# Router and shared-gate logits from two matmul passes, with high and low gate weights side by side in one stationary operand

## The reference, cut to what matters

```
x = x + 0.5 * ffn(layernorm(x))        # first feed-forward
x = x + attention(layernorm(x))        # 16 heads of 128, causal
x = x + 0.5 * ffn(layernorm(x))        # second feed-forward, same weights
```

```
gu = x @ shared_gate_up_w.T ; g, u = split(gu)
shared = sigmoid(x @ shared_gate_w.T) * (silu(g) * u @ shared_down_w.T)
logits = x @ gate_w.T                  # 8 columns; the 9th is x @ shared_gate_w.T
top_w, top_i = top_k(softmax(logits), 2) ; top_w /= sum(top_w)
out = sum over the 2 experts of top_w * expert(x) + shared
```

## Time and profile before

| what | value |
|---|---|
| runs | 551.32, 553.97, 550.83 us |
| profiled execution | 550.31 us in all, span of its instructions 548.4 us |
| TensorE (PE) busy | 518.0 us, 94% of the span, 3318 matmuls |
| weight loads (PEld) busy | 459.2 us, 84% |
| VectorE (DVE) busy | 329.4 us, 60% |
| ScalarE (ACT) busy | 273.7 us, 50% |
| GpSimd (POOL) busy | 274.4 us, 50% |
| mean granted TensorE clock | 0.993 |

### The profile page before, as it was taken

One profiled execution on the slowest core, in us unless ns is written; L12 is line 12 of the kernel. 1 busy time (PEld: TensorE's weight loads), 2 busy tenths in 40 slices (PEclk: granted clock), 3 DMA queues, 4 the chain that ended last, 5 costly groups with the idle time before them and its releaser, 6 DMA issues. The chain is left out here.

```text
span 548.4 us, 10499 instructions
## 1 busy us (share of the span) xinstructions
PE 518.0 (94%) x3318; PEld 459.2 (84%) x3319; DVE 329.4 (60%) x821; ACT 273.7 (50%) x731; POOL 274.4 (50%) x364
## 2 busy tenths in 40 slices
PE   7999699986999999999999999999999899899995
PEld 4787699975898889888988988889889688799985
DVE  6689655558763564655545636646556768755536
ACT  3973355531663553653545525636446465355540
POOL 1738777752656434552654455435532321667750
PEclk9999799999999999999999999999999999999999
DMA  8941233353101002002010020020000140223336
GB/s 284 343 133 30 67 98 106 100 174 76 36 0 59 20 2 77 0 0 76 0 56 21 0 76 0 0 76 0 0 1 0 31 151 2 68 87 104 97 109 210
DMA packets 19401, 37.99 MB, mean 69 GB/s; under 512 B 2864, under 2 KB 10416, under 8 KB 19376
## 3 DMA queue, kind: packets, MB, share of 16 engines
q1 hardware_dynamic: 14960, 25.61, 14.4%
q0 software_dynamic: 4416, 12.06, 6.9%
HBM read 28.49 MB, written 9.18 MB: 69 GB/s over the span
## 5 line engine op out<-in xcount | busy, mean ns | idle before, releaser
L1317 POOL TENSOR_TENSOR s_a<-s_a,rr_a 128x128 f32<-128x128 f32 x64 | 25.6, 401 | 128.3 <-DVE rr_a L1413 128.3
L1353 ACT ACTIVATE s_a<-s_a,mn_a 128x128 f32<-128x128 f32 (+1 forms) x128 | 57.1, 448 | 27.9 <-DVE mn_a L1407 27.0
L179 PE MATMUL bank<-xT_h,area_h 128*128 128x512 f32 x128 | 55.3, 432 | 4.3 <-PEq L1171 3.4
L1403 DVE SCALAR_TENSOR_TENSOR s_a<-bank,cst 128x384 f32<-128x384 f32 x64 | 35.3, 552 | 34.4 <-PE bank L1524 34.4
L1419 DVE SCALAR_TENSOR_TENSOR area_l<-bank,bias_a,area_h 128x256 fp32r<-128x256 f32 x64 | 30.9, 482 | 41.2 <-ACT area_h L1363 41.1
L521 POOL DMA_INDIRECT xn<-x_normed,tok_i_f x46 | 45.7, 994 | 17.2 <-issue 10.5
L1363 ACT ACTIVATE area_h<-bank,bias_a 128x256 fp32r<-128x256 f32 x64 | 30.3, 473 | 42.2 <-PE bank L1552 41.1
L180 PE MATMUL bank<-xT_l,area_h 128*128 128x512 f32 x128 | 50.2, 392 | 0.0
L181 PE MATMUL bank<-xT_h,area_l 128*128 128x512 f32 x128 | 50.2, 392 | 0.0
L1551 PE MATMUL bank<-pT_a,v_a 128*128 128x256 f32 x128 | 39.8, 392 | 4.6 <-ACT pT_a L1358 4.6
L1395 DVE TENSOR_SCALAR qk_a<-bank,bias_a 128x512 f32<-128x512 f32 x32 | 24.0, 751 | 30.5 <-PE bank L181 30.5
(11 more groups left out here) (176 smaller groups left out, 1652.4 us busy)
## 6 DMA issues: line engine op xcount, KB each, us to landing
area<-in_wqkv SPq DMA_DIRECT2D x8, 768.0 KB, 4.4
xn<-y_by_token SPq DMA_DIRECT2D x12, 256.0 KB, 3.7
w_r<-in_w SPq DMA_DIRECT2D x8, 352.0 KB
area_r<-in_w SPq DMA_DIRECT2D x16, 176.0 KB
x_normed<-xn SPq DMA_DIRECT2D x4, 512.0 KB, 5.6
area<-in_wo SPq DMA_DIRECT2D x8, 256.0 KB, 2.7
x_res<-in_x_in SPq DMA_DIRECT2D x4, 256.0 KB, 4.2
wgu_r<-in_wgu SPq DMA_DIRECT2D x4, 256.0 KB
```

The lines of the kernel that those rows point to most:

```text
L179: pe.matmul(psum, lhs[0], rhs[0], start=first, stop=False)
L1353: act.activation(s[b][:, cols], s[b][:, cols], ACT.Exp, bias=mn[:, b, t:t + 1], scale=-1.0, accum_out=rs[:, b, t:t + 1]).then_inc(s_e, 1)
L1403: dve.scalar_tensor_tensor(s[b][:, :], bank[3 + u % 2][:, 0:3 * P], -INV_SCALE, cst[:, C_MASK:C_MASK + 3 * P], ALU.mult, ALU.max).then_inc ...
```

## The change

The gate weights become one tile, `wg_hl`, with four groups of 32 columns for each chunk: high, low, high, zero. Per chunk one matmul takes columns 0 to 63 (high and low side by side) against the high part of x, and one takes columns 64 to 127 (high and zeros) against the low part. Both add into the same 64 partitions of bank 6, so that rows 0 to 8 hold high by high plus high by low, and rows 32 to 40 hold low by high. That makes 4 matmuls per call of `logits`, each with 64 columns in its stationary operand, in place of 6 with 128. ScalarE copies 64 rows in place of 9. `route_turn` is no longer 8 transposes: each is a plain FP32 matmul with the 64x128 block of logits as stationary operand and a 64x9 matrix of zeros and ones as moving operand (`C_SUM`, in the constants), which turns and adds the two row groups in one. The constants grow by 9 columns; VectorE makes low parts for 32 columns per chunk in place of 128.

```diff
+GL = 32
...
-C_N = C_MASK + 3 * P
+C_SUM = C_MASK + 3 * P
+C_N = C_SUM + NG
...
+    for g in range(NG):
+        c[[g, GL + g], C_SUM + g] = 1.0
...
-        wg_h = sbuf("wg_h", [P, KD, P], FP32R)
-        wg_l = sbuf("wg_l", [P, KD, P], FP32R)
+        wg_hl = sbuf("wg_hl", [P, KD, 4 * GL], FP32R)
...
-                        act.activation(flat(wg_h[:, :, :]), wg_raw, ACT.Copy).then_inc(s_gh, 1)
+                        act.activation(wg_hl[:, :, :], wg_raw, ACT.Copy).then_inc(s_gh, 1)
...
-                            act.activation(lgT[2 * half + a][0:NG, :], bank[6][0:NG, a * D:(a + 1) * D],
+                            act.activation(lgT[2 * half + a][0:2 * GL, :], bank[6][0:2 * GL, a * D:(a + 1) * D],
                                            ACT.Copy).then_inc(s_lgt_sb, 1)
...
-                        dve.tensor_tensor(flat(wg_l[:, :, :]), wg_raw, flat(wg_h[:, :, :]).bitcast(FP32),
-                                          ALU.subtract).then_inc(s_gl, 1)
+                        dve.tensor_tensor(wg_hl[:, :, GL:2 * GL], wg_raw[:, :, GL:2 * GL],
+                                          wg_hl[:, :, GL:2 * GL].bitcast(FP32), ALU.subtract).then_inc(s_gl, 1)
...
                         for k in range(KD):
-                            last = split_matmuls(pe, bank[6][:, :], (wg_h[:, k, :], wg_l[:, k, :]),
-                                                 (xT_h[:, k, toks], xT_l[:, k, toks]), k == 0, k == KD - 1)
+                            pe.matmul(bank[6][0:2 * GL, :], wg_hl[:, k, 0:2 * GL], xT_h[:, k, toks],
+                                      start=k == 0, stop=False)
+                        for k in range(KD):
+                            last = pe.matmul(bank[6][0:2 * GL, :], wg_hl[:, k, 2 * GL:4 * GL], xT_l[:, k, toks],
+                                             start=False, stop=k == KD - 1)
                         last.then_inc(s_lgt, 1)
...
                         for j in range(NT):
-                            last = pe.transpose(bank[4][:, j * NG:(j + 1) * NG],
-                                                lgT[j // 2][0:NG, (j % 2) * P:(j % 2 + 1) * P],
-                                                cst[0:NG, C_ID:C_ID + NG])
+                            last = pe.matmul(bank[4][:, j * NG:(j + 1) * NG],
+                                             lgT[j // 2][0:2 * GL, (j % 2) * P:(j % 2 + 1) * P],
+                                             cst[0:2 * GL, C_SUM:C_SUM + NG], start=True, stop=True)
                         last.then_inc(s_logits, 1)
...
-    gate = np.concatenate([a["ffn_gate_w"], a["ffn_shared_gate_w"], np.zeros((P - NG, D), np.float32)], 0)
+    gate = np.concatenate([a["ffn_gate_w"], a["ffn_shared_gate_w"], np.zeros((GL - NG, D), np.float32)], 0)
+    gate = np.concatenate([gate, gate, gate, np.zeros_like(gate)], 0)
```

More of the change, by code:

```diff
@@ L31 @@
 NG = NE + 1
+GL = 32
+assert NG <= GL
 NH, DH = 16, 128
@@ L263, in ffn @@
                 w2_r = area_r[0:IC, :].rearrange("p (e c d) -> p e c d", e=NE, c=2)
-                wg_tile = sb("wg_tile", [P, max(KD * P, TOP_K * NT * NM)])
-                wg_raw = wg_tile[:, 0:KD * P]
+                wg_tile = sb("wg_tile", [P, max(KD * 4 * GL, TOP_K * NT * NM)])
+                wg_raw = wg_tile[:, 0:KD * 4 * GL].rearrange("p (k g) -> p k g", k=KD)
                 tile_hot = wg_tile[:, 0:TOP_K * NT * NM].rearrange("p (a b) -> p a b", b=NM)
@@ L453, in _ @@
                         sp.dma_start(cst[:, 0:C_DESC], consts[:, 0:C_DESC]).then_inc(s_cst, 16)
-                        sp.dma_start(wg_raw, wgate).then_inc(s_gate_in, 16)
+                        sp.dma_start(wg_tile[:, 0:KD * 4 * GL], wgate).then_inc(s_gate_in, 16)
                     for q, (src, raw, _, _) in enumerate(jobs):
@@ L1636 @@
         "consts": constants(),
-        "wgate": chunks(gate.T, D, P).reshape(P, KD * P),
+        "wgate": chunks(gate.T, D, P).reshape(P, KD * 4 * GL),
         "wgu": gu,
```

## The result

The changed kernel takes 554.88 us (median of 17 runs, 553.70 to 558.15); the kernel before, beside it on the same chip, takes 551.80 us (17 runs, 549.27 to 555.17). The ratio is 1.0054 with a 95% interval of 1.0035 to 1.0074: slower by 3.0 us (1.9 to 4.1). The forecast was 552.9 us, 1.8 us slower, in a range of 550.6 to 555.4. The time lies in the range; the sign is right and the size is 1.2 us short. By ratio it sits right on the line of 0.5% between "no change" and "slower".

What follows compares the result with a forecast made beforehand. TensorE was taken to bound the kernel around the turn. Per feed-forward -0.27 (first logits) - 0.08 (second) + 1.26 (turn) = +0.91 us, twice +1.8; from 551.1 that gives 552.9 us, range 550.6 to 555.4.

Steps and rivals of the forecast that it cites:

- What bounds the kernel: TensorE is busy throughout around the route turn, so what it loses or gains there shows at the end.
- Route turn: Sixteen FP32 loads 0.11 us apart plus 0.09 us: 1.85 us for 0.59, so +1.26 us per feed-forward.
- pace of the transposes: Rival at the turn: loads 0.062 us apart, 1.08 us for the turn; +0.3 us in all, 551.4; chance 0.08.
- no load pulled ahead: Rival at the turn: 0.21 us per load, 3.36 us for the turn; +4.8 us in all, 555.9; chance 0.1.
- `logits(1)`: Second logits call: the turn waits for ScalarE's copies, so only 0.08 us is gained per feed-forward.
- `logits(0)`: First logits call: the way in is free, the way out costs 0.19 us; 0.27 us gained per feed-forward.
- shape change by columns: At the logits: each switch between 128 and 64 stationary columns empties the array and costs 0.19 us.
- 0.3 us or more: Sign of shape changes: first matmul of `logits(1)` starts at least this long after its predecessor.
- the first rival: No change of shape by columns at the logits: +1.4 us in all, 552.5 us; chance 0.2.
- a new fall elsewhere: Clock rival: the granted clock falls at another place, giving 556 us; chance 0.04.

Runs made afterwards that it cites:

- e4: Changed kernel with each of the turn's eight FP32 matmuls issued twice; 586.64 us, ratio 1.0165 to the kernel before.
- e8: Changed kernel with all 128 columns in the logits matmuls and all 128 rows in the turn; 586.34 us, ratio 1.0095 to the kernel before.
- e2: Changed kernel with narrow logits kept, but the turn by transposes and VectorE adding the halves; 576.71 us, ratio 0.9964 to the kernel before.
- e6: Changed kernel with the turn two matmuls later in `shared_up(3)`; 581.96 us, ratio 1.0031 to the kernel before.
- e5: Changed kernel unaltered, timed again on another chip; 584.28 us, ratio 1.0072 to the kernel before.
- e3: Changed kernel with 64 moving columns in place of 9 at the turn; 579.70 us, ratio 1.0029 to the kernel before.
- e12: Kernel before, unaltered, profiled again on another chip; 577.75 us in one execution.
- e7: Changed kernel with narrow logits, turn by transposes, VectorE adding the halves, turn two matmuls later; 577.73 us, ratio 0.9953 to the kernel before.
- e9: Changed kernel with 64 moving columns at the turn and each turn matmul issued twice; 586.97 us, ratio 1.0151 to the kernel before.

## Why the prediction was nearly right, and what was mis-sized

That the time lies in the range is luck in part. The upper bound of 555.4 us was built from dearer loads and dearer shape changes, which did not come. What did come, a fall of the clock behind the turn, was in no term of the sum, and as a rival it stood outside the range (556); with it behind both turns in every execution the sum would be 551.1 + 4.6 = 555.7 us, outside.

- **What bounds the kernel: right.** The turn and the work around it set the end. f0's delay came to the first expert product in full behind an unchanged wait of 4.14 us, as the steps of the earlier trace rows said. That part of it went again in this execution, between 61 and 120 us, is due to where the low clock lay.
- **Route turn: right.** 1.88 us for 1.85, 0.111 us a load for 0.11, and 0.09 us beyond the loads as predicted (e4); 0.07 of these go when the operand has all 128 rows (e8). The rivals "pace of the transposes" (1.08 us) and "no load pulled ahead" (3.36 us) fell. The Trainium skill, "Perfetto Trace Analysis", section Transposes, asks to do a logical transpose with the transpose operation and not with a standard matmul. The runs agree and give the price: 1.88 against 0.64 us for the same eight blocks (the changed kernel and e2).
- **`logits(1)`: right.** From the first matmul of `shared_up(2)`'s second group to the turn, 4.31 us became 4.22, so 0.09 us were gained (0.08 predicted), and TensorE now waits 0.30 and 0.26 us for ScalarE. e6 shows the lost 0.3 us by getting it back.
- **`logits(0)`: the shape change by columns, which I priced at 0.19 us, costs nothing.** From the first logits to the first matmul behind them it took 1.44 us and takes 0.93, 0.51 us less and not 0.27; and the first matmul of `logits(1)` starts 0.23 us behind its predecessor (23.29 to 23.52), where the prediction had named 0.3 us or more as its sign. I had carried the loss of the earlier trace rows, where rows change, over to columns. This was the first rival (chance 0.2), and it makes the work +0.7 us per feed-forward in place of 0.91: +1.4 in all. The rule of the Trainium skill that I weighed there ("TensorEngine Tiling (Array Packing)", section Key Properties: a change of the tiling mode drains the engine) is not borne out for 64 columns: the loads at 23.29 and 24.20 run ahead of their matmuls. No row says whether an operand of 64 columns puts the array in another mode at all. For 64 rows the rule agrees with the earlier trace rows. The prediction put the delay behind the turn down to the shape too; e8 and the attention's rows show that most of it stands there at full shape as well. It is there before and after the change, so the sum does not suffer.
- **The clock: the term that was missing, +1.6 us.** I had given "a new fall elsewhere" a chance of 0.04 as a mishap. It belongs to the change: 16 loads in a row, with nearly nothing behind each, are followed by a stretch at half clock in 6 of 12 cases, 1.6 us each. With a rate of a half that is 2 x 0.5 x 1.6 = +1.6 us, and 1.4 + 1.6 = 3.0 us is what was measured. How well the two agree is chance: the rate comes from twelve cases in four versions of the turn and on four chips, only two of them on the chip of the result; at a quarter or three quarters the sum would be 2.2 or 3.8 us, and e5 points to a higher rate on its chip. What is shown is that transposes have no such fall in 8 cases, what one fall costs, and that e5 lost more to the clock than before in all its executions together. So the two errors were of opposite sign, -0.4 and +1.6 us, and the forecast of +1.8 came 1.2 us short.
- **Open.** Whether the number of moving columns changes anything at a single turn (e3 had no fall in two cases, which half a chance gives one time in four; its time is that of the work alone, and by the mean clocks its twelve executions lost 0.8 us less to the clock than before, give or take 3); what decides within one program whether the clock falls; what e8 loses beside its work and the clock; and the fall at 133 us, which the first chip's trace of before has not and which I took for chance (in e12, the kernel before too falls once ahead of the attention, at 144 us).

## What to carry to other kernels

Count the weight loads before you replace a transpose by a 0/1 matmul: eight FP32 transposes of 128-column blocks are 8 loads 0.06 us apart, eight FP32 matmuls are 16 loads 0.11 us apart, and however few columns move, the loads set the pace. A gain ahead of a wait is worth something only if the waiting step moves too: e7 keeps the cheap half of the change, adds the halves on VectorE, puts the wait two matmuls later, and is 0.5% faster than before where the change is 0.5% slower. And where an edit puts a run of almost empty matmuls into a stretch at full clock, read the granted clock behind it in several executions, for one execution may show the fall or not.

## What the runs showed of the hardware

- A stationary operand of 64 columns in place of 128 neither speeds up nor disturbs the stream of 512-column matmuls (0.228 us each, loads pulled ahead). Going to 64 rows costs something (0.32 us to the turn's first start in e6 where 0.23 is the pace), but giving the turn all 128 rows saves only 0.1 us (e8). The first FP32R matmul behind FP32 ones is followed late at full shape too: 0.30 us where 0.12 is the pace (142.18 us in the kernel before).
- The single FP32 turn is followed by half clock in 6 of 12 cases and the doubled one in 6 of 6, with TensorE busy throughout. It begins 1.1 to 1.4 us behind the end of a single turn, 0.8 to 1.2 us behind a doubled one in f0 and in the last microsecond of a doubled one in f1 (e4: from 471.8, where the turn ends at 472.46). It lasts 3.4 us, behind two of the doubled turns (e4 and e9, both in f1) 6.8, and then costs twice as much. Behind the transposes it did not appear in 8 cases.
- The same program takes 551.8 us on one chip and 578 to 581 on three others, while its front stage agrees to 0.01 us (e12, on one of the three). The difference lies in the expert stages: from the first up product of a feed-forward's experts to the last they take 48.5 and 46.0 us on the first chip, 61.2 and 59.3 in e12, with the attention between them equal. These windows of the kernel before show the first of the two stages, on the first chip and in e12: from 60 to 125 us, TensorE's row counts 438 matmuls against 365, with a granted clock of 0.95 against 0.88 and 118 against 80 GB/s.

```profile
60.00:125.00 65.00, 63.36 (x438) 60.33 (x439) 33.96 (x87) 32.87 (x98) 43.68 (x44) 0.95 0.37 118
```

```profile
60.00:125.00 65.00, 59.32 (x365) 54.69 (x366) 25.77 (x69) 28.46 (x91) 38.19 (x40) 0.88 0.25 80
```
